# Two layers of adaLN blocks on one core: coupling product once, mask on GpSimd, a new order table

## What is computed

```
global: gf = sigmoid(MLP(mean over tokens of h))
out = h
for _ in range(3):                                  # layer 0, cycles
    tf = sigmoid(gelu(gelu(gelu(out @ w1 + b1) @ w2 + b2) @ w3 + b3) @ w4 + b4)
    coupling = 0.1 + adaptive_range * (0.7 * gf + 0.3 * tf - 0.5) * 2.0
    out = out + coupling * twist(out)               # twist swaps and negates quarters of the features

term1 = where(mask, 0, qc_s @ vu.T)                 # layer 1, mask = above the diagonal
lookahead = where(mask, sigmoid(qu_s @ ku.T), 0)
Su = term1 @ lookahead.T
scores = where(mask, -max, qc_s @ kc.T - silu(Su))
out = softmax(scores) @ vc
```

## Time and profile before

| | us |
|---|---|
| median of 3 runs | 2122.74 |
| lowest, highest | 2122.28, 2125.06 |
| the profiled execution | 2121.46 |
| its span in the trace | 2120.2 |
| busy PE, DVE, ACT, POOL | 2038.9, 1050.6, 995.5, 641.3 |

### The profile page before, as it was taken

The page is one execution under the profiler, slowest core; times in us unless marked ns, Lnnn a source line. Parts: engine busy times, 40 slices in busy tenths (PEclk is TensorE's granted clock), DMA queues, the critical chain, the costliest instruction groups (busy, mean ns, idle before and its releaser), DMA issues. The chain is left out here.

```text
span 2120.2 us, 31087 instructions
## 1 busy us (share of the span) xinstructions
PE 2038.9 (96%) x11544; PEld 1348.0 (64%) x11544; DVE 1050.6 (50%) x2888; ACT 995.5 (47%) x2092; POOL 641.3 (30%) x724
## 2 busy tenths in 40 slices
PE   6659999999999999999999999999999999999998
PEld 4425655755665575556556655655677678888887
DVE  4424555646454665646466555667443447223221
ACT  1315565656557556555755565565444531111111
POOL 1102322422232332323233332323243323333332
PEclk9779999999999999999999999999999999999999
DMA  3100001001000100000010000001311133333333
GB/s 104 70 10 13 1 1 35 21 1 36 1 21 1 35 11 11 20 16 21 1 36 11 12 11 26 21 1 56 131 31 53 18 91 73 72 77 76 77 78 65
DMA packets 59017, 76.70 MB, mean 36 GB/s; under 512 B 7075, under 2 KB 52654, under 8 KB 58614
## 3 DMA queue, kind: packets, MB, share of 16 engines
q1 hardware_dynamic: 42640, 56.29, 8.0%
q0 software_dynamic: 12288, 16.79, 4.7%
q10 hardware_dynamic: 3942, 1.65, 0.3%
HBM read 53.58 MB, written 21.00 MB: 35 GB/s over the span
## 5 line engine op out<-in xcount | busy, mean ns | idle before, releaser
L1770 POOL TENSOR_TENSOR s<-s,ri 128x256 f32<-128x256 f32 (+3 forms) x128 | 162.5, 1272 | 487.3 <-DVE ri L1546 475.0
L809 PE MATMUL bank<-hT,wqkv 128*128 128x512 f32 x640 | 304.6, 611 | 1.1 <-ACT hT L1105 1.1
L1261 ACT ACTIVATE h<-bank 128x512 f32<-128x512 f32 x128 | 76.4, 597 | 344.9 <-PE bank L1021 335.2
L1021 PE MATMUL bank<-xin,ew 128*128 128x256 f32 x1024 | 237.6, 383 | 0.0
L1034 PE MATMUL bank<-ew,h 128*128 128x256 f32 x1024 | 230.6, 383 | 0.0
L1034 PEld LDWEIGHTS bank<-ew,h 128*128 128x128 f32 x1024 | 196.2, 192 | 31.7 <-issue 4.9
L1021 PEld LDWEIGHTS bank<-xin,ew 128*128 128x128 f32 x1024 | 189.7, 191 | 28.7 <-issue 5.6
L809 PEld LDWEIGHTS bank<-hT,wqkv 128*128 128x128 f32 x640 | 115.6, 192 | 129.7 <-issue 129.0
L1238 ACT ACTIVATE s<-s,mn 128x128 f32<-128x128 f32 (+3 forms) x256 | 141.6, 554 | 119.7 <-DVE mn L1540 118.2
L1808 POOL DMA_INDIRECT out<-y,indices x64 | 102.9, 1608 | 285.1 <-DVE y L1689 199.8
L876 PE MATMUL bank<-look,term 128*128 128x384 f32 (+3 forms) x512 | 175.6, 452 | 0.3 <-POOL look L1754 0.3
(11 more groups left out here) (240 smaller groups left out, 3633.4 us busy)
## 6 DMA issues: line engine op xcount, KB each, us to landing
ew<-L_ffn_w SPq DMA_DIRECT2D x24, 1024.0 KB
x<-L_attn_x SPq DMA_DIRECT2D x8, 512.0 KB, 3.9
x_scratch<-x SPq DMA_DIRECT2D x8, 512.0 KB, 2.9
x1s<-x_scratch SPq DMA_DIRECT2D x8, 512.0 KB
out<-x1s SPq DMA_DIRECT2D x8, 512.0 KB, 2.9
xn_scratch<-n_xn SPq DMA_DIRECT2D x8, 512.0 KB, 3.0
wqkv<-L_wmod SPq DMA_DIRECT2D x2, 1536.0 KB, 9.9
wqkv<-w_qkv SPq DMA_DIRECT2D x1, 3072.0 KB, 10.1
```

The lines of the kernel that those rows point to most:

```text
L809: mm = te.matmul(banks[i][:, :], b1.wqkv[:, kk, j * CH1 + hp * P:j * CH1 + (hp + 1) * P], b1.hT[:, kk, :], start=(kk == 0), stop=(kk == KC ...
L1021: mm = te.matmul(banks[i][:, f * 2 * P:(f + 1) * 2 * P], w1[:, kk, (2 * n + f) * P:(2 * n + f + 1) * P], xin[:, kk, :, :].rearrange("p h s ...
L1770: g.tensor_tensor(sc, sc, b1.ri[u % 2][:, :].unsqueeze(2).to_broadcast([P, 2, w]), ALU.mult).then_inc(s["weighted"], 1)
```

## The change

- The coupling product is linear. With h' = h + tf x twist(h), h' @ w1 = h @ w1 + tf x (twist(h) @ w1), and twice twisted is minus the input. So `cn1` runs in cycle 0 only, and a new step `twist` makes twist(h) @ w1 with a negated copy of half of w1 (`turned`), 4 products 128x512. ACT copies both from the banks into the space of q (`straight`, `twisted`); the sums of cycles 1 and 2 (`hidden`, in the space of pT) come from DVE behind `cn4`, and ACT takes GELU from there. DVE's operations behind `cn4` are 13, 9 and 5 in the cycles 0, 1 and 2, where they were 5 each; `hT` is still carried on, and `cn4`'s tanh waits for it since `tf` now lies in the space of a score tile.
- The sign of the twist goes into w1, g1 and the layer-0 columns at setup.
- The mask product is gone. After DVE's (1 + th) x bank a select on GpSimd puts 1e30 above the diagonal of the diagonal tile of `th` (`masked`), and `sc`'s vector step waits for it.
- `su` is term x lookahead alone; `qc` x `w`, tanh, vector step and the select are a step `sw`.
- `PERIOD` is a new table. In `first_steps` a round is sc0:n, wt0:n-1, tp0:n-2, pv0 instead of pv0, tp0, wt0, sc0.
- The beginning: q,k,v weights go first on ACT's queue and the other 20 loads of `w0_load` to SP's; `wmod` is loaded in two parts (4 and 8 of its 12 column groups) and `cols` split alike; the second part of the columns, the rows and `setup0` stand behind q,k and inside the block attention; layer 1's columns and rows stand in the coupling cycles, its large weight load behind them; DVE's casts for iota and `sel` become three in a step `tables` behind cn4 of cycle 1.

Core of the diff:

```diff
-        steps = [("wt0", b, n - 1)] if 0 <= n - 1 < NBLK else []
-        if n < NBLK:
-            steps.append(("sc0", b, n))
+        if n < NBLK:
+            yield [("sc0", b, n)]
+        if 0 <= n - 1 < NBLK:
+            yield [("wt0", b, n - 1)]
+        if 0 <= n - 2 < NBLK:
+            yield [("tp0", b, n - 2)]
...
@@ PERIOD @@
-    +cn3:1 su:8 sc:8 attend:6 turn:7 +cn4:1 w:2.0 attend:7 proj:3.0 proj:3.3 +cn1:2 weigh:8 o_out:1 su:9 sc:9 +cn2:2
+    attend:7 sw:9 +cn1:2 proj:3.0 proj:3.3 o_out:1 +cn2:2 +cn3:2 sc:9 turn:8 weigh:9 su:10 sw:10 +cn4:2 proj:3.1
...
+    order = [("wqkv_load", 0, 0), ("mod_load", 0, 0), ("x0", 0, 0), ("mod_load", 0, 1), ("w0_load", 0, 0), ("mod_load", 1, 0),
+             ("mod_load", 1, 1), ("silu", 0, 0), ("stats", 0, 0), ("norm", 0, 0), ("cols", 0, 0), ("setup", 0, 0)]
+    beside = {("kq", 0, 1): [("cols", 0, 1)], ("v", 0, 0): [("rows", 0, 0), ("ga0_load", 0, 0)],
+              ("tp0", 0, 1): [("setup0", 0, 0)], ("tp0", 0, 5): [("silu", 1, 0)], ("norm", 0, 1): [("cols", 1, 0)],
+              ("cn4", 0, 0): [("cols", 1, 1)], ("cn1", 0, 1): [("rows", 1, 0), ("w1_load", 0, 0)],
+              ("cn4", 0, 1): [("tables", 0, 0)]}
...
@@ TensorE, su @@
-                mm = te.matmul(banks[i][:, col + t * P:col + w], c_.identb[:, :], c_.above[:, :], start=False,
-                               stop=(t == 0))
...
@@ TensorE, twist @@
+                te.matmul(banks[i][:, :], b0.turned[:, c * P:(c + 1) * P], b0.hT[:, 0, :], start=True, stop=False)
+                te.matmul(banks[i][:, :], b0.w1[:, 0, c * P:(c + 1) * P], b0.hT[:, 1, :], start=False, stop=True
+                          ).then_inc(full[i], 1)
...
@@ ACT, cn1 of cycles 1 and 2 @@
+                a.wait_ge(s["combined"], KC * ((CYCLES - 1) * b + n - 1) + c + 1)
+                a.activation(b0.a1[:, c, :], b0.hidden[c], ACT.Gelu, bias=b0.b1[:, c:c + 1]).then_inc(s["activated"], 1)
...
@@ DVE, cn4 @@
+            if n < CYCLES - 1:
+                for j in range(KC):
+                    v.tensor_tensor(b0.a1[:, j, :], tf, b0.twisted[j], ALU.mult).then_inc(done, 1)
...
+                    v.tensor_tensor(b0.hidden[j], (b0.straight, b0.hidden)[n][j], b0.a1[:, j, :], ALU.add
...
+            if n == 0:
+                    v.tensor_tensor(b0.straight[j], tf, b0.straight[j], ALU.mult).then_inc(done, 1)
+                    v.tensor_tensor(b0.twisted[j], b0.twisted[j], b0.straight[j], ALU.subtract).then_inc(done, 1)
...
@@ GpSimd, sw @@
+            diagonal = b1.th[u % 2][:, :, t * P:(t + 1) * P]
+            g.affine_select(out=diagonal, in_=diagonal, compare_op=ALU.is_ge, fill=BIG, base=0,
+                            pattern=[[0, 2], [-1, P]], channel_multiplier=1).then_inc(s["masked"], 1)
...
@@ DVE, sc @@
-            for which in range(su_banks(t)):
-                i, nth = at["su", b, n, which]
-                v.wait_ge(drained[i], nth)
+            v.wait_ge(s["masked"], g + 1)
```

327 lines of the change are left out of this document (192 added, 135 removed).

## The result

| | before | after |
|---|---|---|
| median, us | 2122.78 (4 runs, 2122.28 to 2125.06) | 2070.51 (4 runs, 2066.95 to 2075.78) |
| profiled execution (span) | 2121.46 (2120.2) | 2075.78 (2074.3) |
| ratio after to before | | 0.9754, 95% interval 0.9729 to 0.9779 |

The change takes 52 us off. The forecast was 2074, 3.5 above the median, in a range from 2048 to 2100. A sum can come out right with wrong terms, so the two traces are cut at the same points and compared piece by piece. TensorE bounds the kernel outside the beginning, so a piece ends where TensorE starts layer 1 of a batch.

A forecast was written before the change was run, and what follows sets the result against it. TensorE's issue was taken to bound the kernel after the beginning, a chain through all engines within it. 2121.5 - 55 (work) + 21 (waits) - 14.5 (beginning) = 2073, median 1.3 higher: 2074 us; range 2048 to 2100.

The forecast's parts named there:

- Coupling products: TensorE, batches 1 to 7: 8 coupling products a batch for 12, 0.86 us each, 24.1 us less.
- Mask products: TensorE: 256 mask products out, 0.17 us a pair for 96 units and 0.22 for 32, 23 us less (14 to 31).
- Changes of array shape: TensorE: 44 fewer changes of array shape outside the beginning at 0.19 us each, 8 us less (0 to 9).
- Waits: Steady stretch: new TensorE waits at three short places, 3 us a batch (1.1 to 5), 21 us back (8 to 35).
- The first place: Cycle 2: cn3 waits for cn2's GELU, 0.8 to 1.0 us a batch; cn2 behind cn4, 0 to 0.9 more.
- The second and third: Cycle 0: sc:7's bank waits behind cn4's 13 vector operations, 0 to 1.5 us; head pair's end: GpSimd select, 0.3 to 1.5.
- rival 1: No wait appears, so all 55 + 14.5 us arrive: 2053 us, period 181 to 182; chance 0.12.
- 7 x 3: Batches 1 to 7: waits of 3 us in each, 21 us back in the sum.
- Rival 3: Slower: DVE's block bounds if two-input operations take 1.0 us beside GpSimd's masks; 2137 us at 12 us a batch; chance 0.05.
- Rival 2: Waits eat the work saved: steady waits of 7 us a batch, 2107 us; chance 0.07.
- Beginning: Before layer 1 of batch 0: earlier loads -21, setup0 +6, twist +4, cycles +1 and -4.5; -14.5 us (-8 to -22).
- The tail: The experts' tail from 1664 us on has the same products; change put at zero.

The follow-up runs named there:

- mask_on_pe: The changed kernel with the mask back on TensorE as 256 products of 128 columns and no select on GpSimd; 2082.2 us, 0.9816 of the kernel before.
- dve_block_longer: The changed kernel with four more unused vector operations behind cn4's block of cycle 0 in batches 1 to 7; 2102.1 us, 0.9913 of the kernel before.
- the second profile: The changed kernel itself run once more without any edit; 2067.2 us (5 runs), 0.9746 of the kernel before.
- coupling_each_cycle: The changed kernel with cn1 multiplied in each of three cycles, no twist, five vector operations behind every cn4; 2150.2 us, 1.0129 of the kernel before.

## Why the prediction was right, and where it wasn't

- **What bounds the kernel** was right. There are two regimes, and after the beginning it is TensorE's issue: in the steady periods each product put back cost its own time, and more.
- **Coupling products.** 0.86 us each was right (18.0 for 17.2 in five batches).
- **Mask products.** 0.09 each foretold, 0.084 measured in place (the text's upper bound takes 0.18 for the 32 units that it prices at 0.22; that is 1 us). But 23 us in all became 13 in mask_on_pe. The term left out that the select has a price in idle where little stands beside it: at the end in the new table, in the steady periods too in the old one, where no gain clear of the noise is left.
- **Changes of array shape: mis-sized.** 5.7 for five batches foretold; all that isn't coupling, mask, wait or clock is 2.7. That is 0.09 for each of 30 changes at the most, not 0.19, and no kernel isolated it. The 0.19 was read on a change into products of 64 rows. Counted in the traces over the five periods, all changes fall from 449 to 419, but those into 64 rows or fewer stay at 155. The price was read on a kind of change that doesn't fall out.
- **Waits: the term that was mis-sized.** "Together 1.1 to 5 us a batch; I take 3, in the middle since no row shows the places themselves." It was 1.0 a batch. The first place was right to the tenth: from the start of cn2's last record to cn3 it takes 1.37 us for 0.43 without a wait, 0.94 in each batch. The second and third cost nothing in the steady stretch; dve_block_longer shows that the second ends just in time, with some 0.5 us to spare. The middle of a range is not a reading. The text also took 189 for the period before, from two periods of which one was the 189.8; the others have 188.1. The period of 182.2 lies beside the 181 to 182 that the text had set as the sign for rival 1, which is thus nearly what happened in that stretch.
- **What covered it up.** "7 x 3" was spread evenly over the batches. Instead six periods wait about 1 us each and the last one 9.6, where the rounds of the choice fill DVE. I had walked through one ordinary batch and not through the one that carries extra work. In sum TensorE's idle rose by 13 us outside the beginning (19.5 to 32.4), for 21 foretold. The clock gave 1.5 us that the sum didn't have (the low stretches there cost 14.8 before and 13.3 after, by the estimate above), and the work fell by some 48, for 55. The waits were put 8 too high and the work 7 too high, and these two cancel: that the three pieces came out at -36.5 for -34 is in good part luck.
- **Rival 3** was wrong as a forecast and right as a mechanism. Its block of vector operations is on the path: 3.5 us more of it cost 3.6, and 5.3 with the clock. Its threshold ("it decides from 10 us of waits a batch on") is a division of the gain that no run tests; the operations took 0.69 to 0.79 us in the mean, not 1.0. Where they meet GpSimd both are slower, GpSimd by more: its operation on look takes 1.52 us beside the block at 446.14 and 0.40 at 1396.31, and the block's last two 0.98 and 0.88 for 0.69. The Trainium skill, GPSIMD Engine Reference, section 1, Specifications, says that GpSimd's SBUF interfaces are shared with VectorE, with contention when a vector instruction has two SBUF inputs. These rows agree.
- **Rival 2's figure** doesn't follow from its condition: 7 us of waits a batch put the text's own sum at 2053 + 49 = 2102, not 2107. Either lies outside the range and nothing else hangs on it.
- **Beginning.** -14.5 foretold, bounds -8 and -22; -9.4 and -17.7 measured. By steps, with the second profile: q,k at 16.4 (foretold 16.0); the first score product 21.8 earlier (21); the attention 9.1 longer, of which some 6.5 for setup0 (6) and 2.5 for the order of blocks (0, give or take 3); cn1 to cn2 1.7 longer (4); cycle 0 to 1 3.2 shorter (1 longer); cycle 1 to 2 5.7 shorter (4.5); ahead of cn1 and behind the last cn2 0.8 and 1.5 longer, where the sum had nothing. The clock is what the sum didn't have: 8 us between two profiles of one kernel. Both profiles lie inside the bounds, but steps inside them miss: cycle 0 to 1 by 4.2, and the attention by 3.1 the other way.
- **The tail** at zero was right for the experts. From the first product of the last attention on it took 641.4 to 643.0 for 641.4, although 32 mask products left it.
- **Open.** Why mask_on_pe, with the old masks in the new table, still waits 8.3 us in the last period where the kernel before has 3.2. The table moves the start of the choice's rounds on DVE (16 rounds in 51 us for 60), but no kernel had that alone. No kernel has the new table with both old products either, so what the order is worth by itself isn't known.

## What to carry to other kernels

When an order is written out by hand, an edit has no price of its own: the mask alone gave 3 us at most and perhaps nothing, the product alone taken back made the kernel slower than before, and together in a new order they gave 2.5%. Price the work by rows, and the waits by walking through the exact rows of each short place, to the tenth; also through the batch with extra work, where they turned up. A step moved takes all its engines along, so look at what stands behind it on each, above all at which function ACT's neighbours need.

## What the runs showed of the hardware that was not expected

- In dve_block_longer an idle of 2.63 us of TensorE was followed by the lower clock in six of seven batches, at 1.6 to 1.9 us each. In coupling_each_cycle one of 2.83 was in five of seven, and one of 1.47 in one of seven. The waits of 0.78 us of the changed kernel were not (granted clock 1.00 from 200 to 1360). The kernel before has a stretch at 0.96 from 600 to 640 without any idle, which made one of its periods 189.8.
- The clock early in the program comes in two patterns for the same kernel: full up to 40 us, or 0.83 from 20 to 40.
- The idle shown ahead of a product is 0.2 us less than what the wait costs: 0.78 shown for 0.94 lost, 2.63 for 2.83. Where it falls between two products of 64 rows that would run side by side it costs another 0.8.
- One more alternation of GELU and exponential on ACT costs 2 x 1.31 us of its time; ACT at 61% busy had no room for it in that place.
